# Expert tiles that gather their own token rows, begun four blocks earlier at five per block

## The chip, the cores and the metric

The kernel runs on one core of a Trainium2 chip. Its time is the device time of one execution in microseconds (us); the time before is the median of three runs. The core's engines are TensorE (PE, matrix products and transposes), VectorE (DVE), ScalarE (ACT), GpSimd (POOL) and the queue engine SyncE (SP). Each takes its own instructions in order and waits on semaphores that the others raise. TensorE's clock is granted at one of two levels, 1.2 and 2.4 GHz; the profile shows the granted share, 1.0 being 2.4 GHz.

## What is computed

```
xn = layernorm(x)                               # x: (2, 4096, 256) f32
out = x + mamba(xn) + moe(xn)

mamba: r = xn * rsqrt(mean(xn^2) + eps) * norm_w
       x_s, z = split(r @ in_proj.T)            # 512 channels each
       u = silu(causal_conv4(x_s) + conv_b)
       dt, B, C = split(u @ x_proj.T)           # 16 states
       delta = softplus(dt @ dt_proj.T + dt_b)
       h_t = exp(delta_t * A) * h_(t-1) + delta_t * u_t * B_t      # for each t, channel, state
       y = (C_t . h_t + u * D) * silu(z);  out_proj(y) + xn

moe:   logits = xn @ gate.T                     # 8 experts, hidden 512
       the two best experts of each token, each with a masked softmax weight
       moe = sum over the two of weight * w2 @ (silu(w1 @ xn) * (w3 @ xn))
```

All is f32. There are 8192 tokens, 64 tiles of 128.

## The kernel before

**Blocks.** The sequence is cut into blocks of 256 tokens, `(j, b)` with j = 0 to 15 and b the batch, 32 in all, numbered `number(j, b)` = 2j + b. A block has 32 steps v: a step handles one state s and one half of the channels. Blocks 0 to 7 and 28 to 31 are written out, those between are one hardware loop (`run`) whose round is two blocks. At each step ACT makes `exp(delta * A)` for the next step (`make_da`, two buffers), POOL makes `du * B` three steps ahead (`make_dbu`, a ring of eight), DVE scans (`scan`, two instructions of 256), PE transposes the states two steps behind (`transpose_h`) and DVE adds them, weighted with C, four steps behind (`add_state`).

**Work beside the steps.** The projections of the next block and the output of the block before stand at fixed steps of the `SLOTS` table, on each engine between the instructions of the recurrence: z at 0 and 1, y at 4 and 5, the output product at 8, `xs` at 10 and 12, two convolution pairs at 13 and 15, x_proj at 18, dt at 20 and 21, softplus from 22 to 28. POOL's part of the softplus (`w_minus_1` and `correction` at step 26, `make_delta` and `make_du` at 28) must end before the first `make_dbu` of the next block (at 29). `residual` on ACT (step 9) scales a second copy of the raw x block; SP loads it by `reload_x`, at step 8. `result` on DVE (step 11) adds that to the output product.

**Experts, routing.** In block 0, `normalise_all` on DVE makes the layer norm of all 64 token tiles in SBUF (`xall`): eight pairs before the first scan (NPRE), the other 24 one pair a step; `dispatch_T` (PE, ACT) transposes each tile and `dispatch_logits` makes its logits. At block 1, step 3 (ROUTE), `route` and `place` on DVE choose two experts per token and give each of the 16384 (token, choice) pairs a slot in an order sorted by expert, padded so that each tile of 128 slots has one expert. `eid` holds the expert of each slot tile. 135 tiles can be in use.

**Experts, dispatch.** From block 1, step 8 POOL sends one token tile each step by an indirect DMA (`dispatch`, L432) into `xbuf` in DRAM, 128 in all; with each row go the token's number and its weight. `xbuf` was filled with empty rows before (`clear`, 68 stores), as was the expert output `moe_dram` (33 stores).

**Expert tiles.** `tiles_at` places 12 tiles in two blocks (PER), from block 6 on (J0 = 3) to block 28. A tile that starts at step t has its transpose at t (XT), its copy and H1 at t + 2, H3 at t + 3, tanh at t + 4, DVE's two products (`tile_a2`, `tile_ha`) and Y at t + 5, the weighted copy (YO) at t + 7, and at t + 9 an adding indirect DMA on POOL to `moe_dram` (L445). Before it, `load_tile` on SP has brought its rows and their `meta` from `xbuf`; `load_weights` brings the expert's weights for the tile four further on. The weights lie where `xall` was. `add_result` on POOL at last adds `moe_dram` to `out`, one block each third step from block 28, step 26.

**Parameters.** ACT's queue loads all small weights; the two bias rows `dt_b` and `conv_b` are loaded element by element into a row of `dtT`. DVE's first product on a weight (L1064) waits for all nine of these loads.

## Time and profile before

| | us |
|---|---|
| median of 3 runs (lowest, highest) | 2923.68 (2920.98, 2927.97) |
| the profiled execution | 2921.28 |
| its span, first to last instruction | 2919.5 |
| PE busy, weight loads busy | 2437.7, 2049.5 |
| DVE busy | 2467.5 |
| ACT busy | 1504.8 |
| POOL busy | 2001.6 |

The predictions' sums are made against the profiled execution. A busy time is the union of an engine's instructions; on PE they are pipelined and overlap. In the rows below, a group row gives the line, engine and operation, out<-in with shapes and count, then busy time and mean ns of one, then the idle time just before them and what ended it. A timeline row gives start, duration, engine, line and operation, and in brackets the idle time before it and what ended that. The lines are those of the kernel printed above.

### The profile page before, as it was taken

The page shows a single profiled execution, that of the slowest core. Times are in us where ns is not written, and L with a number is a line of the kernel's source. Part 1 is how long each engine was busy: PE and PEld are TensorE (multiplying, and loading weights), DVE is VectorE, ACT ScalarE, POOL GpSimd, SP SyncE. Part 2 cuts the span into 40 slices and gives each one's busy share as a digit, 9 for nine tenths or more (in the row PEclk, how much of TensorE's full clock was granted, in tenths as well). Part 3 has the DMA queues.
Part 4 walks back from the last instruction along what each step waited for, and adds up shares of the span by engine and source line. Part 5 has one row for each costly group of instructions (what it writes and reads, how often), then busy time and mean ns, then how long its engine had stood idle before and what let it go on. Part 6 is the DMA issues. An engine that isn't in the chain of part 4 may idle for free.

```text
span 2919.5 us, 50661 instructions
## 1 busy us (share of the span) xinstructions
PE 2437.7 (83%) x14442; PEld 2049.5 (70%) x14442; DVE 2467.5 (85%) x3901; ACT 1504.8 (52%) x3675; POOL 2001.6 (69%) x1467
## 2 busy tenths in 40 slices
PE   2876655579999899999999989899898999997775
PEld 2864544458788778787778877788787777775554
DVE  6979777798899888898888898888898887998997
ACT  1444444455555555455555555555465554565553
POOL 3346999985777766677766777666676666777873
PEclk8757766779999999999999999999999999997776
DMA  7442432244565555464555565555564554542431
GB/s 219 120 106 80 155 104 75 75 143 129 161 180 148 158 168 156 143 189 142 163 162 148 160 174 158 155 167 147 159 174 137 168 163 147 175 119 53 78 75 36
DMA packets 316127, 406.46 MB, mean 139 GB/s; under 512 B 44296, under 2 KB 207496, under 8 KB 315800
## 3 DMA queue, kind: packets, MB, share of 16 engines
q1 hardware_dynamic: 284448, 359.49, 40.3%
q0 software_dynamic: 28144, 43.01, 8.1%
q8 instruction: 133, 2.18, 0.3%
q14 instruction: 194, 1.59, 0.2%
q10 hardware_dynamic: 3208, 0.19, 0.1%
HBM read 332.59 MB, written 78.39 MB: 141 GB/s over the span
## 4 chain that ended last, share of the span: by engine, by line
PE 48%; POOL 16%; DVE 15%; issue 11%; DMA 4%; ACT 4%; SPq 2%; ACTq 0%; DVEq 0%; POOLq 0%
PE HT L1246 9%; POOL h L468 7%; DVE h L1015 6%; PE G L1288 5%; PE G L1295 5%; PE FA L1205 4%; PE FB L1205 4%; PE G L1302 4%; DVE yT L1030 3%; DMA xraw<-in_x_dram 3%; PE FA L1172 3%; POOL xbuf L432 3%; PE FA L1311 2%; PE FB L1172 2%; POOL tmpA L476 2%
## 5 line engine op out<-in xcount | busy, mean ns | idle before, releaser
L468 POOL TENSOR_TENSOR h<-du,bbc 128x512 f32<-128x512 f32 x1024 | 1356.8, 1412 | 786.9 <-PE HT L1246 750.2
L1015 DVE TENSOR_TENSOR_SCAN h<-DA,carry,h 128x256 f32<-128x256 f32 x2048 | 1416.5, 733 | 196.1 <-ACT DA L716 83.5
L716 ACT ACTIVATE DA<-delta,alog 128x256 f32<-128x256 f32 x2048 | 891.4, 469 | 589.2 <-DVE h L1015 516.1
L1246 PE MATMUL HT<-ident,h 128*128 128x128 f32 x4096 | 687.8, 302 | 356.0 <-DVE yT L1030 329.1
L1246 PEld LDWEIGHTS HT<-ident,h 128*128 128x128 f32 x4096 | 514.9, 154 | 502.0 <-issue 359.1
L1030 DVE SCALAR_TENSOR_TENSOR yT<-HT,cT,yT 128x512 f32<-128x512 f32 x960 | 698.2, 727 | 187.8 <-PE HT L1246 187.3
L1288 PE MATMUL G<-xtT,W 128*128 128x128 f32 x2160 | 287.8, 290 | 0.0
L1288 PEld LDWEIGHTS G<-xtT,W 128*128 128x128 f32 x2160 | 274.5, 206 | 2.9
L1295 PE MATMUL G<-xtT,W 128*128 128x128 f32 x2160 | 263.8, 275 | 0.0
L1302 PE MATMUL G<-W,fill 128*128 128x256 f32 x1080 | 257.7, 381 | 3.3 <-DVE fill L991 3.3
L1295 PEld LDWEIGHTS G<-xtT,W 128*128 128x128 f32 x2160 | 252.8, 192 | 0.0
L445 POOL DMA_INDIRECT moe_dram<-W,meta x135 | 213.8, 1584 | 21.2 <-issue 18.6
L1302 PEld LDWEIGHTS G<-W,fill 128*128 128x128 f32 x1080 | 194.6, 190 | 28.0 <-DVE fill L991 4.9
L1172 PE MATMUL FB<-xrT,inT 128*128 128x256 f32 x512 | 154.1, 455 | 11.3 <-DVE inT L1064 11.3
L476 POOL TENSOR_SCALAR tmpA<-tmpB 128x1024 f32<-128x1024 f32 x32 | 129.7, 4054 | 42.0 <-ACT tmpB L690 42.0
L432 POOL DMA_INDIRECT xbuf<-W x128 | 129.7, 1013 | 21.3 <-issue 19.9
L1172 PEld LDWEIGHTS FB<-xrT,inT 128*128 128x128 f32 x512 | 115.5, 233 | 30.7 <-DVE inT L1064 11.7
L1311 PE MATMUL FA<-outT,zs 128*128 128x256 f32 x512 | 130.1, 412 | 0.8 <-DVE zs L1046 0.8
L1205 PE MATMUL FB<-xs,cwd 128*128 128x256 f32 x512 | 127.7, 391 | 0.0
L1205 PE MATMUL FA<-xs,cwd 128*128 128x256 f32 x512 | 127.7, 391 | 0.0
L1172 PE MATMUL FA<-xrT,inT 128*128 128x256 f32 x512 | 123.3, 384 | 0.0
L1311 PEld LDWEIGHTS FA<-outT,zs 128*128 128x128 f32 x512 | 104.7, 210 | 17.2 <-DVE zs L1046 1.0
(169 smaller groups left out, 2694.7 us busy)
## 6 DMA issues: line engine op xcount, KB each, us to landing
W<-in_w_T_dram SPq DMA_DIRECT2D x405, 512.0 KB, 4.9
bbc<-b_dram SPq DMA_DIRECT2D x256, 256.0 KB, 5.2
xbuf<-fill SPq DMA_DIRECT2D x68, 258.0 KB, 8.5
W<-xbuf SPq DMA_DIRECT2D x135, 128.0 KB
xraw<-in_x_dram SPq DMA_DIRECT2D x64, 256.0 KB, 6.3
W<-in_x_dram SPq DMA_DIRECT2D x32, 256.0 KB, 7.1
out_dram<-tmpA SPq DMA_DIRECT2D x32, 256.0 KB
moe_dram<-fill SPq DMA_DIRECT2D x32, 256.0 KB
```

The lines of the kernel that those rows point to most:

```text
L432: pool.indirect_dma_start(xbuf[:, :], bass.IndirectOffsetOnAxis(ap=slot[:, i:i + 1], axis=0), xall[:, i % TILES, :], None).then_inc(s_disp ...
L468: pool.tensor_tensor(h[:, v % RING], du[:, b, 2 * q:2 * q + 2, :], bbc[:, s // 2 % BRING, s % 2, :].unsqueeze(1).to_broadcast([P, 2, T]), ...
L716: i = act.activation(DA[:, v % 2, k, :], delta[:, b, c, :], ACT.Exp, scale=nega[:, c, s:s + 1])
L1015: i = dve.tensor_tensor_scan(h[:, v % RING, k, :], DA[:, v % 2, k, :], h[:, v % RING, k, :], carry[:, b, s, c:c + 1], ALU.mult, ALU.add)
L1030: i = dve.scalar_tensor_tensor(out=yT[:, b, k, :], in0=HT[:, k, :], scalar=cT[:, b, k, s:s + 1], in1=yT[:, b, k, :], op0=ALU.mult, op1=ALU ...
L1172: i = pe.matmul(dst[:, c, :], inT[:, k, at:at + P], xrT[:, b, k, :], start=(k == 0), stop=(k == KD - 1))
L1205: i = pe.matmul(dst, cwd[:, c, k, :], xs[:, c, k:k + T], start=False, stop=(k == TAPS - 1))
L1246: i = pe.transpose(HT[:, k, c * P:(c + 1) * P], h[:, (2 * s + c // 2) % RING, c % 2, k * P:(k + 1) * P], ident[:, :])
L1288: i = pe.matmul(G[:, 0, f * P:(f + 1) * P], w1[:, k % WSLOTS, c, f * P:(f + 1) * P], xtT[:, c, :], start=(f == 0 and c == 0), stop=(c == K ...
L1295: i = pe.matmul(G[:, 1, f * P:(f + 1) * P], w3[:, k % WSLOTS, c, f * P:(f + 1) * P], xtT[:, c, :], start=(f == 0 and c == 0), stop=(c == K ...
L1302: i = pe.matmul(G[:, 0, 0:DM], ha[:, f * P:(f + 1) * P], w2[:, k % WSLOTS, f, :], start=(f == 0), stop=(f == IC - 1))
L1311: i = pe.matmul(FA[:, t, :], zs[:, c, t * P:(t + 1) * P], outT[:, c, :], start=(c == 0), stop=(c == CH - 1))
```

## The change

The tokens' rows are no longer sent to `xbuf`. The normalised rows, each with the token's two weights, are stored in order to `xn_dram` (eight stores of 1 MB), and each tile gathers its 128 rows from there. For that the kernel inverts the slot table: slot = 128 * hi + lo; for each of the 128 (tile, choice) columns q DVE makes a one-hot row of lo (128 wide) and a one-hot row of hi (136 wide) times the token number, and PE accumulates their product over all q in PSUM, so that entry (lo, hi) holds the token number plus one, plus 8192 for a second choice, and 0 for an empty slot. Seven small DVE operations make indices and first/second masks of it. POOL copies each tile's index column (`choose`), gathers (`gather`, an indirect DMA with a read index) and later scatters by the same column. ACT makes each tile's weights from two 1-wide products.

The tiles begin in block 2 (J0 = 1), five a block (PER = 10 in two blocks), with five weight buffers instead of four; the last five tiles stand in block 28. All stages shift: index 0, gather 1, transpose 5, H1 7, H3 8, tanh 9, products and Y 10, YO 12, scatter 14. The hardware loop now runs 12 rounds (j = 2 to 13) instead of 10. `reload_x` moves from step 8 to step 6. `normalise_all` moves from DVE to ACT, with two pairs ahead of the first step. The two bias rows are loaded by SP after `in_proj`, and DVE's first product waits for `norm_w` only. `add_result` starts at block 29, step 18, each second step.

```diff
@@ constants
-    ZSTEP = 2
+    ONEHOTS = 8
-    J0 = 3
-    PER = 12
-    WSLOTS = 4
+    J0 = 1
+    PER = 10
+    WSLOTS = 5
-    META = 4
+    META = 5
-    NPRE = 8
-    LOW_TILES = TILES + TILES // 2
+    NPRE = 2
...
-        ADD_FROM = 26
+        ADD_FROM = 50
...
-            return at // 3 if at >= 0 and at % 3 == 0 and at // 3 < 2 * JB - 1 else None
+            return at // 2 if at >= 0 and at % 2 == 0 and at // 2 < 2 * JB - 1 else None
...
-        XT, XT_COPY, H1, H3, TANH, A2, MULT, Y, YO, SCATTER = 0, 2, 2, 3, 4, 5, 5, 5, 7, 9
-        W1_LOAD, W3_LOAD, W2_LOAD = 6, 7, 9
+        INDEX, GATHER = 0, 1
+        XT, XT_COPY, H1, H3, TANH, A2, MULT, Y, YO, SCATTER = 5, 7, 7, 8, 9, 10, 10, 10, 12, 14
+        W1_LOAD, W3_LOAD, W2_LOAD = 11, 12, 14
@@ SP
+            sp.wait_ge(s_id, 10)
+            sp.dma_start(cb_row.rearrange("o (c p) -> o c p", p=P),
+                         conv_b.rearrange("p c -> c p").unsqueeze(0), allow_slow_non_contiguous=True).then_inc(s_bias, 16)
+            sp.dma_start(dtT[ROWS:KDT, :].rearrange("o (c p) -> o c p", p=P),
+                         dt_b.rearrange("p c -> c p").unsqueeze(0), allow_slow_non_contiguous=True).then_inc(s_bias, 16)
             load_all(1)
...
+            def store_normalised():
+
+                sp.wait_ge(s_gate, 2)
+                for g in range(TILES // 8):
+                    sp.dma_start(xn_rows[g], xall[:, 8 * g:8 * g + 8, :]).then_inc(s_xnd, 16)
...
-                    if v == SLOTS["transpose"] and prv:
+                    if unit(j, b, v) < TILES // ZROWS:
+                        clear(unit(j, b, v))
+                    if due("normalise", v - 1) and prv:
                         reload_x(*prv)
...
+                    if unit(j, b, v) == U + ROUTE + 1:
+                        store_normalised()
+                        sp.wait_ge(s_xnd, 16 * (TILES // 8))
+                        sp.wait_ge(s_slot, 1)
+                        for g in range(WSLOTS):
+                            first_weights(g)
@@ POOL
-            def dispatch(i):
...
+            def choose(g, r):
+
+                if isinstance(g, int) and g == 0:
+                    pool.wait_ge(s_idx, 1)
+                pool.tensor_copy(token[:, r:r + 1], at_col(index, g)).then_inc(s_ix, 1)
+
+            def gather_ready(g):
+                pool.wait_ge(s_ix, g + 1)
+                if not isinstance(g, int) or g > 1:
+                    pool.wait_ge(s_xtr, g - 1)
+                    pool.wait_ge(s_gt, 2 * (g - 1))
+
+            def gather(g, k):
...
+                pool.indirect_dma_start(xt[:, k % 2, :], None, xn_dram[:, :],
+                                        bass.IndirectOffsetOnAxis(ap=token[:, k % META:k % META + 1], axis=0)).then_inc(s_xt[k % 2], 16)
...
                     if at := tiles_at(j, b, v, SCATTER):
                         scatter_ready(at[0])
+                    if at := tiles_at(j, b, v, GATHER):
+                        gather_ready(at[0])
...
-                    i = unit(j, b, v) - U - DISPATCH
-                    if 0 <= i < 2 * TILES:
-                        dispatch(i)
+                    if at := tiles_at(j, b, v, GATHER):
+                        gather(at[0], at[1])
+                    if at := tiles_at(j, b, v, INDEX):
+                        choose(at[0], at[1] % META)
@@ ACT
+            def normalise_all(i):
+
+                for q in range(NT * i, NT * i + NT):
+                    act.activation(xall[:, q, 0:DM], xall[:, q, 0:DM], ACT.Identity, bias=at_col(nm, q),
+                                   scale=at_col(rstd, q)).then_inc(s_nrm, 1)
...
+                    act.activation(weight[:, r, 0:1], xt[:, k % 2, DM + 1:ROW], ACT.Identity,
+                                   scale=at_col(second_of, g)).then_inc(s_gt, 1)
+                    act.wait_ge(s_gt, 2 * g + 1)
+                    act.activation(weight[:, r, 1:2], xt[:, k % 2, DM:DM + 1], ACT.Identity, bias=weight[:, r, 0:1],
+                                   scale=at_col(first_of, g)).then_inc(s_gt, 1)
@@ DVE
+            def invert():
+
+                for q in range(2 * TILES):
+                    wait(dve, s_inv, q - ONEHOTS + 1)
+                    dve.tensor_scalar(onehot[:, q % ONEHOTS, 0:P], its[:, 0:P], lo[:, q:q + 1], None,
+                                      ALU.is_equal).then_inc(s_oh, 1)
+                    dve.tensor_scalar(onehot[:, q % ONEHOTS, P:P + SLOTTED], its, hi[:, q:q + 1], tokv[:, q:q + 1],
+                                      ALU.is_equal, ALU.mult).then_inc(s_oh, 1)
+                dve.wait_ge(s_inv, 2 * TILES)
...
-            dve.wait_ge(s_par, NPAR)
+            dve.wait_ge(s_nw, 16)
...
                     if second(j, b) and v == ROUTE:
                         route()
                         place()
+                        invert()
@@ PE
+            def invert():
+
+                for q in range(2 * TILES):
+                    pe.wait_ge(s_oh, 2 * q + 2)
+                    pe.matmul(INV, onehot[:, q % ONEHOTS, 0:P], onehot[:, q % ONEHOTS, P:P + SLOTTED],
+                              start=(q == 0), stop=(q == 2 * TILES - 1)).then_inc(s_inv, 1)
```

## Rows read from the trace of the kernel before

**Rows 1.** The page: busy time by engine; TensorE's granted clock in 40 slices, tenths.

```profile
PE 2437.7 (83%) x14442; PEld 2049.5 (70%) x14442; DVE 2467.5 (85%) x3901; ACT 1504.8 (52%) x3675; POOL 2001.6 (69%) x1467
...
PEclk8757766779999999999999999999999999997776
```

**Rows 2.** Timeline of DVE: `result` (L1054) of blocks 0, 1, 4 and 27.

```profile
252.15 0.68 DVE L1054 TENSOR_TENSOR tmpA<-FA,xraw 128x512 f32<-128x512 f32 x1
...
337.94 0.68 DVE L1054 TENSOR_TENSOR tmpA<-FA,xraw 128x512 f32<-128x512 f32 x1
...
610.67 0.68 DVE L1054 TENSOR_TENSOR tmpA<-FA,xraw 128x512 f32<-128x512 f32 x1
...
2622.12 0.68 DVE L1054 TENSOR_TENSOR tmpA<-FA,xraw 128x512 f32<-128x512 f32 x1
```

**Rows 3.** Groups of instructions: the scans, the state sums, a tile's second product.

```profile
L1015 DVE TENSOR_TENSOR_SCAN h<-DA,carry,h 128x256 f32<-128x256 f32 x2048 | 1416.5, 733 | 196.1 <-ACT DA L716 83.5
...
L1030 DVE SCALAR_TENSOR_TENSOR yT<-HT,cT,yT 128x512 f32<-128x512 f32 x960 | 698.2, 727 | 187.8 <-PE HT L1246 187.3
...
L991 DVE TENSOR_TENSOR fill<-fill,G 128x512 f32<-128x512 f32 x135 | 92.8, 688 | 18.2 <-PE G L1295 5.6
```

**Rows 4.** Stretches: block 0, routing, six tiles, none: us, busy (count), clock, DMA, GB/s.

```profile
90.00:100.00 10.00, 10.00 (x51) 10.00 (x50) 10.00 (x17) 5.26 (x13) 2.54 (x2) 0.50 0.46 123
...
196.00:233.00 37.00, 3.83 (x21) 3.25 (x21) 33.67 (x107) 4.76 (x10) 4.38 (x4) 0.57 0.00 0
...
839.00:926.00 87.00, 81.35 (x516) 70.14 (x515) 76.12 (x118) 48.58 (x119) 60.67 (x44) 0.96 0.58 164
...
2758.00:2833.00 75.00, 56.18 (x261) 42.13 (x261) 67.80 (x105) 40.35 (x101) 58.42 (x48) 0.77 0.39 72
```

**Rows 5.** Timelines of SP, ACT, DVE around step 10 of block 14.

```profile
1380.07 0.37 SPq L306 DMA_DIRECT2D xraw<-in_x_dram  x1
...
1387.45 1.09 ACT L598 ACTIVATE xraw<-xraw,nm,onep 128x256 f32<-128x256 f32 x2 [5.06 <-DMA xraw<-in_x_dram]
...
1389.34 1.39 DVE L1015 TENSOR_TENSOR_SCAN h<-DA,carry,h 128x256 f32<-128x256 f32 x2 [2.11 <-ACT DA L716]
```

**Rows 6.** Timelines of PE in block 13 and DVE in block 14, steps 13 to 18.

```profile
1307.92 1.95 PE L1295 MATMUL G<-xtT,W 128*128 128x128 f32 x16
...
1310.42 2.00 PE L1205 MATMUL FB<-xs,cwd 128*128 128x256 f32 x8
...
1405.94 0.75 DVE L1030 SCALAR_TENSOR_TENSOR yT<-HT,cT,yT 128x512 f32<-128x512 f32 x1 [3.51 <-PE HT L1246]
...
1413.64 0.75 DVE L1030 SCALAR_TENSOR_TENSOR yT<-HT,cT,yT 128x512 f32<-128x512 f32 x1 [3.11 <-PE HT L1246]
```

**Rows 7.** POOL: ends of its chain in block 16; groups of its indirect DMAs.

```profile
1606.79 4.23 POOL L476 TENSOR_SCALAR tmpA<-tmpB 128x1024 f32<-128x1024 f32 x1
...
1621.09 2.50 POOL L468 TENSOR_TENSOR h<-du,bbc 128x512 f32<-128x512 f32 x2 [0.43 <-ACT carry L723]
...
L445 POOL DMA_INDIRECT moe_dram<-W,meta x135 | 213.8, 1584 | 21.2 <-issue 18.6
...
L432 POOL DMA_INDIRECT xbuf<-W x128 | 129.7, 1013 | 21.3 <-issue 19.9 <-POOL tmpA L481 0.6 <-POOL W L430 0.3
```

**Rows 8.** Start and block 0: DVE and SP timelines; last, who waited for whom.

```profile
27.75 1.42 DVE L1064 TENSOR_SCALAR inT<-inT,nw 128x1024 f32<-128x1024 f32 x2 [15.77 <-DMA dtT<-in_conv_b_dram]
...
31.28 0.39 DVE L1071 TENSOR_SCALAR xpT<-xpT 128x64 f32<-128x64 f32 x3
...
71.72 7.08 DVE L875 TENSOR_SCALAR W<-W 128x256 f32<-128x256 f32 x16
...
80.02 0.70 DVE L875 TENSOR_SCALAR W<-W 128x256 f32<-128x256 f32 x2
...
8.58 22.08 SPq L348 DMA_DIRECT2D W<-in_x_dram  x24
...
ACT W L567 <- PE G L1154: 53.1, 25, 5.3
```

More of the change, by code:

```diff
@@ L184, in build @@
         gate = scratch[1][:, 0:2 * TILES]
-        slot = scratch[6][:, 512:512 + 2 * TILES].bitcast(mybir.dt.uint32)
+        onehot = W[:, part + 4 * 1024:part + 4 * 1024 + ONEHOTS * (P + SLOTTED)].rearrange("p (r c) -> p r c", r=ONEHOTS)
+        hi, lo, tokv = [scratch[1][:, at:at + 2 * TILES] for at in (128, 256, 384)]
+        hi_i = scratch[1][:, 512:512 + 2 * TILES].bitcast(mybir.dt.int32)
+        slot_i = scratch[1][:, 640:640 + 2 * TILES].bitcast(mybir.dt.int32)
+        its = scratch[2][:, 0:SLOTTED]
+        idxf, index, second_of, first_of = [scratch[0][:, at * SLOTTED:(at + 1) * SLOTTED] for at in range(4)]
+        index = index.bitcast(mybir.dt.uint32)
+        INV = G[:, 1, 0:SLOTTED]
         LG = G[:, 1, :].rearrange("p (t e) -> p t e", e=E)
@@ L583, in normalise @@
                 act.wait_ge(s_x, 16 * (n + 1))
-                if isinstance(n, int) and n == EARLY:
-                    act.wait_ge(s_stats, LATE_MOMENTS + NEWTON + FINISH)
                 wait(act, s_delta, n)
@@ L738, in front @@
                 ln_dt(j, b)
-            for dst, src in ((nw, norm_w), (dpar, D_par)):
-                act.dma_start(dst[:, :], src).then_inc(s_par, 16)
+            act.dma_start(nw[:, :], norm_w).then_inc(s_nw, 16)
             act.dma_start(cw[:, :, :], conv_w.rearrange("(c p) o k -> p c (o k)", p=P)).then_inc(s_par, 16)
@@ L761, in _ @@
             make_da((0, 0), 0)
+            act.wait_ge(s_stats, LATE_MOMENTS + NEWTON + FINISH)
+            for i in range(NPRE):
+                normalise_all(i)
             def step(j, b):
@@ L870, in tables @@
                 chain(dve.tensor_scalar(onep[:, to], yy[:, 0, to], 1.0, None, ALU.add))
-            def normalise_all(i):
-                for q in range(NT * i, NT * i + NT):
-                    dve.tensor_scalar(xall[:, q, 0:DM], xall[:, q, 0:DM], at_col(mean, q), at_col(rstd, q),
-                                      ALU.subtract, ALU.mult).then_inc(s_nrm, 1)
             done = 0
@@ L931, in route @@
                 link(dve.reciprocal(gate[:, :], twice))
-                link(dve.tensor_copy(xall[:, :, DM + 1], gate[:, 0:TILES]))
+                for w in range(2):
+                    dve.wait_ge(s_route, done)
+                    dve.tensor_copy(xall[:, :, DM + w], gate[:, w * TILES:(w + 1) * TILES]).then_inc(s_gate, 1)
             def place():
@@ L964, in place @@
                 link(dve.tensor_reduce(where, rank.rearrange("p (e q) -> p q e", e=E), AX.X, ALU.add))
-                dve.tensor_copy(slot[:, :], where).then_inc(s_slot, 1)
-                its = scratch[2][:, 0:SLOTTED]
+                link(dve.tensor_copy(slot_i, where))
+                link(dve.tensor_single_scalar(hi_i, slot_i, 7, ALU.logical_shift_right))
+                link(dve.tensor_copy(hi, hi_i))
+                link(dve.scalar_tensor_tensor(out=lo, in0=hi, scalar=-float(P), in1=where, op0=ALU.mult, op1=ALU.add))
                 dve.wait_ge(s_iota, 2)
                 cmp = W[:, part + 5 * 1024:part + 5 * 1024 + SLOTTED * E].rearrange("p (i e) -> p i e", e=E)
+                link(dve.tensor_copy(tokv, tokens[:, :]))
                 link(dve.tensor_copy(its, eid[:, :]))
@@ L1091, in _ @@
             tables(EARLY * NT, TILES)
-            for i in range(NPRE):
-                normalise_all(i)
             def step(j, b):
```

137 lines of the change are left out of this document (58 added, 79 removed).

## The prediction

> **What bounds the kernel now.** I read the page first, then the length of a block, then single steps. The page [rows 1] has VectorE (DVE) busy 85% and TensorE (PE) 83% of the span, neither full. DVE's `result`, once per block, cuts the run [rows 2]: four blocks with dispatch take (610.67 - 252.15) / 4 = 89.6 us, the 23 up to 2622.12 take 2011.5, 87.5 each (six expert tiles; 88.1 without the first, which began late), and the last four steps of this clock take 288. A block without tiles is 75 us [rows 4]. A tile thus costs 13.1 / 6 = 2.2 us.
>
> Step by step (a block has 32 steps, one per scan pair) most steps last exactly what DVE needs: two scans and one `add_state`, 1.94 us from start to start [rows 3]. So DVE's order is the path, and a block is 32 x 1.94 = 62, nine other DVE operations of 0.6 = 5.4, six tiles x 1.4 for their two products [rows 3] = 8.4, together 75.9, and some 12 us of named stalls:
> - At step 10 the scan waits 2.11 us for ACT, which sat 5.06 us at `residual` until `xraw` had landed; SP had issued it 7.4 us before [rows 5]. About 1.6 a block on average (odd blocks lose 1.2).
> - At steps 16 and 18 `add_state` waits 3.51 and 3.11 for PE's transposes, which stand behind a convolution pair (2.55 per channel, 5.1) and a tile's H3 (1.8) [rows 6].
> - At the end POOL's chain of six operations sets the next scan: 1606.79 to 1622.4 = 15.6 [rows 7].
> Every second block adds about 3 more where the hardware loop closes.
>
> **The change, part by part.** The sum goes against the profiled execution: 2921.28 us, span 2919.5; the median of the runs shown is 2923.68, 2.4 above it.
>
> *Start.* The two bias rows go from ACT's queue to SP's, and DVE waits for `norm_w` alone. Before, DVE idled 15.8 us for them [rows 8]. That isn't all won: SP must now issue some 7 us of tiny rows ahead of 30 loads of x, whose 24 last took it 22.08 us [rows 8], so the statistics end not before about 46 instead of 54.7. At most 8.7; it could also cost 7, if the bias rows land late for the first convolution. I take 5. Sixteen normalisations leave DVE before the first scan (7.08 [rows 8]); four take their place on ACT at 0.5 each (two in 1.00, 1387.45 to 1388.45 [rows 5]), and the logits chain starts earlier by about 3.5. In block 0, 60 normalisations (30 us) come to ACT; they lie beside 53.1 us in which ACT waited for PE's transposes [rows 8]. PE is 100% busy there at a granted clock of 0.50, its 1.2 GHz level [rows 4], so PE, not DVE, sets that block, and nothing is won by freeing DVE. Some steps had no such wait: I charge 1.5 (0 to 8). Together -7 (-16 to +8). The lighter clearing (34 stores for 101) lies in SP's slack: 0.
>
> *Block 1.* Routing keeps its 37 us of DVE alone [rows 4] plus five small operations (1.2). The inversion is new: 128 pairs of DVE comparisons, 128 and 136 wide, with one and two per-partition scalars, and one f32 product each on PE; nothing else of the recurrence runs beside it, since DVE takes its orders in turn. One-scalar price: 1.42 / 2 = 0.71 for 1024 wide; three of 64 take 0.39, or 0.13 each [rows 8], so 0.6 ns an element, and 128 wide is 0.71 - 0.54 = 0.18. Two-scalar price: 0.70 / 2 = 0.35 for 256 wide, less 120 elements = 0.28. Sum 0.46 x 128 = 59. PE at its low clock makes 51 passes in 10.00 us [rows 4]; two passes a product, a little wider, are 0.42, 54 us, hidden just under DVE. Ends: 0.13 each gives 33; 0.44 each (16 in 7.08) gives 113; I take 59 as the nearest forms give it. With the 1.8 of the tail: +62, less 1.5 of dispatch before `result`: +60. SP meanwhile waits for 8.5 MB of stores and issues 7.9 MB of weights. At 200 GB/s that is some 82 us after the gates at 217, hence about 299, and the inversion ends near 295: hidden, barely.
>
> The Trainium skill (VectorE: DVE Perf Modes, The TRN2 errata) charges an SBUF operation 58 cycles plus half its f32 width, and nothing for scalars read per partition; by it the pair is 0.26 us and the inversion 33. The three narrow operations above start about 0.10 apart, where it says 0.094, so for immediates the trace agrees; the wider rows with such scalars lie above it, which is why the sum does not use it.
>
> *Block 1 to block 2.* 85.8 before [rows 2]. Dispatch (24 to 32 operations a block of 1.013 and their gaps [rows 7]) is gone, one tile's product comes: 75 + 2.5 = 77.5, so -8.3.
>
> *Blocks 2 to 28, five tiles each.* Four terms against the mean of 88.0:
> - `reload_x` moves two steps up, before the tile's weights: issue to residual grows from 7.4 to about 12 us, the wait goes. -1.6. Next late is PE's output product, which just fits.
> - PE: tiles now run H1/H3 at 7/8, 13/14, 19/20, 26/27, 0/1. A step's transposes may start 2.5 us late before `add_state` notices. At step 13 stand H1 and a convolution pair, 0.44 + 1.8 + 5.1 on a backlog of 1: stall at 16 +0.7. H3 no longer stands at 18: -1.6. At steps 0 and 1 H1, H3 and z together need 8 us against 3.9 + 2.5: just late, but the old stall there goes, -0.7 in all with small change. -1.6.
> - DVE: outside steps 26 to 31 four tiles' products before and after: 0. Inside, one pair (1.4) goes, but POOL sets that stretch.
> - POOL: gather and scatter both fall on step 26, behind the two long operations and ahead of the products that the next block needs. A gather's issue is unknown: 1.01 (plain) to 1.58 (adding) [rows 7]; I take 1.1. 1.1 + 1.58 + gaps = +2.9 on the chain; the scatter that stood ahead of it at 25 (1.57) goes, and the rest is slack of the chain: the stretch goes from 17.2 to 18.2, +1.0.
> Sum -2.2, less 0.5 since fewer bursts meet the loop's end: 85.3. Bounds: 83 (the chain hides the gather) to 88 (nothing but the reload gained, gather at 1.58 and late for PE). 26 such intervals to block 28's `result`: 26 x 85.3 = 2218 against 2622.12 - 337.94 = 2284.2: -66 (-126 to +4). The two extra loop rounds are in it. The choosing copies on POOL (0.3, five a block) and ACT's two 1-wide products per tile (0.6) lie beside waits; without cover 5 x 0.9 = 4.5 a block.
>
> *End.* One more tile's remains in blocks 28 and 29 and adds packed at every second step: 288 becomes 292.5, +4.5.
>
> Sum: -7 + 60 - 8.3 - 66 + 4.5 = -16.8: span 2902.7, execution 2904.5, and about 2906 beside the median. About 0.2% (6 us) is what a measurement can tell from no change.
>
> **Rivals.**
> - *Work is conserved (slower).* 135 tiles cost 2.2 wherever they stand, and POOL's gather on the end-of-block chain gives back what the reload wins, so blocks stay at 88: 26 x 88 = 2288, +4 instead of -66; total about 2976. For it: the tile's cost is mostly DVE's own 1.4, and POOL's chain is tight. It decides from 86 us a block (26 x 0.7 = 18). Against: the reload's wait is plain.
> - *Bursts were the cost.* With 5 tiles PE needs 5.5 less a block and its stalls at 16 and 18 shrink to those of a bare block: 82.7 a block, total about 2838. For: PE 81 busy of 87 [rows 4]. Against: 13/14 meets both convolutions.
> - *Dear inversion.* 0.44 an operation, as when POOL worked beside DVE [rows 8]: +54, total about 2960. Against: POOL is idle here.
> - *Cheap inversion.* 0.13 an operation, as for immediates: 33, PE at full clock: about 2880. It is what the errata rule of the Trainium skill would give.
> - *Late gather.* Issued 7 us into step 26 it must land by PE's step 30, 6 us on; scatters took 6.5 to land. Each us late past PE's slack is 27 us. Counted in the 88. The Trainium skill (DMA: Bandwidth & Descriptors, Anatomy of one DMA) fits 2.0 us plus bytes, 2.3 here; no gather is in this trace.
>
> **How the numbers follow.** Forecast 0.42 (2882 to 2930), conserved 0.22, bursts 0.16, dear 0.08, cheap 0.12. Range 2850 to 2968. Faster: 0.42 x 0.75 + 0.16 + 0.12 + a little of conserved = 0.61; same 0.10; slower 0.29.
>
> **What would show it.** The gap between the routing and the next scan: 61 (right), 35, or 115. `result` to `result` 85.3 mean in the middle. ACT's wait for `xraw` near 0 and no scan stall at 10; 4.3 at 16, 1.5 at 18. POOL from the first long operation to the next block's first product 18 to 19 us. PE waiting for the gathered tile: none. Blocks at 88 or more, or an inversion over 80, make the forecast wrong.

## The result: slower, where the prediction said slightly faster

The changed kernel takes 2981.05 us (median of 4, 2972.32 to 2983.86), the kernel before 2924.52 (median of 4, 2920.98 to 2927.97): a ratio of 1.0191, 95% interval 1.0168 to 1.0215. The prediction was 2906, in a range of 2850 to 2968. The profiled execution of the changed kernel has a span of 2982.0 us, 62.5 above the 2919.5 of before.

### The profile page after: what moved, and what is told of

Read it like the earlier page. It is cut to its first block, busy times and chain, and to the rows that moved or that the text cites. A ratio compares the mean times of both kernels' runs of the same rounds, so it can differ in the third digit from the quotient of the medians.

```text
span 2982.0 us, 52444 instructions
## 1 busy us (share of the span) xinstructions
PE 2512.3 (84%) x14698; PEld 2146.5 (72%) x14698; DVE 2498.1 (84%) x4105; ACT 1595.0 (53%) x4009; POOL 2031.3 (68%) x1607
## 4 chain that ended last, share of the span: by engine, by line
PE 58%; POOL 18%; DVE 14%; issue 7%; ACT 2%; DVEq 0%; SPq 0%; POOLq 0%; DMA 0%; ACTq 0%
PE HT L1284 10%; PE G L1333 8%; DVE h L1055 7%; PE G L1340 6%; POOL h L477 6%; PE G L1347 5%; PE FB L1243 4%; PE FA L1243 4%; PE FB L1210 4%; PE FA L1356 4%; POOL tmpA L485 4%; POOL delta L496 2%; DVE yT L1070 2%; POOL tmpA L490 2%; PE G L1315 2%
## 5 line engine op out<-in xcount | busy, mean ns | idle before, releaser
L477 POOL TENSOR_TENSOR h<-du,bbc 128x512 f32<-128x512 f32 x1024 | 1370.7, 1456 | 815.4 <-PE HT L1284 754.6
L1284 PE MATMUL HT<-ident,h 128*128 128x128 f32 x4096 | 673.3, 295 | 318.0 <-DVE yT L1070 308.1
L1284 PEld LDWEIGHTS HT<-ident,h 128*128 128x128 f32 x4096 | 511.1, 151 | 442.2 <-issue 248.6
L1333 PE MATMUL G<-xtT,W 128*128 128x128 f32 x2160 | 358.1, 335 | 59.5 <-ACT xtT L634 59.5
L1333 PEld LDWEIGHTS G<-xtT,W 128*128 128x128 f32 x2160 | 339.8, 247 | 67.6 <-ACT xtT L634 65.9
L1340 PE MATMUL G<-xtT,W 128*128 128x128 f32 x2160 | 274.1, 282 | 0.0
L1340 PEld LDWEIGHTS G<-xtT,W 128*128 128x128 f32 x2160 | 265.4, 200 | 0.0
L454 POOL DMA_INDIRECT moe_dram<-W,token x135 | 217.9, 1614 | 37.2 <-issue 37.2
L445 POOL DMA_INDIRECT W<-xn_dram,token x135 | 139.6, 1034 | 20.9 <-issue 6.9
L1210 PE MATMUL FB<-xrT,inT 128*128 128x256 f32 x512 | 150.5, 447 | 0.8 <-ACT xrT L618 0.8
L648 ACT ACTIVATE fill<-G 128x512 f32<-128x512 f32 x135 | 80.1, 593 | 130.7 <-PE G L1333 130.7
L485 POOL TENSOR_SCALAR tmpA<-tmpB 128x1024 f32<-128x1024 f32 x32 | 116.6, 3643 | 31.2 <-ACT tmpB L711 31.2
L1210 PEld LDWEIGHTS FB<-xrT,inT 128*128 128x128 f32 x512 | 117.4, 238 | 20.2 <-issue 1.1
L1210 PE MATMUL FA<-xrT,inT 128*128 128x256 f32 x512 | 122.5, 382 | 0.0
L1356 PE MATMUL FA<-outT,zs 128*128 128x256 f32 x512 | 120.6, 390 | 0.8 <-DVE zs L1086 0.8
```

Of the source, the lines that this page charges most:

```text
L477: pool.tensor_tensor(h[:, v % RING], du[:, b, 2 * q:2 * q + 2, :], bbc[:, s // 2 % BRING, s % 2, :].unsqueeze(1).to_broadcast([P, 2, T]), ...
L485: pool.tensor_scalar(tmpA[:, :, :], tmpB[:, :, :], 1.0, -1.0, ALU.add, ALU.add).then_inc(s_wm, 1)
L1210: i = pe.matmul(dst[:, c, :], inT[:, k, at:at + P], xrT[:, b, k, :], start=(k == 0), stop=(k == KD - 1))
L1284: i = pe.transpose(HT[:, k, c * P:(c + 1) * P], h[:, (2 * s + c // 2) % RING, c % 2, k * P:(k + 1) * P], ident[:, :])
L1333: i = pe.matmul(G[:, 0, f * P:(f + 1) * P], w1[:, k % WSLOTS, c, f * P:(f + 1) * P], xtT[:, c, :], start=(f == 0 and c == 0), stop=(c == K ...
L1340: i = pe.matmul(G[:, 1, f * P:(f + 1) * P], w3[:, k % WSLOTS, c, f * P:(f + 1) * P], xtT[:, c, :], start=(f == 0 and c == 0), stop=(c == K ...
```

## The profile after

The page of the changed kernel, busy times and TensorE's granted clock, beside [rows 1]:

```profile
PE 2512.3 (84%) x14698; PEld 2146.5 (72%) x14698; DVE 2498.1 (84%) x4105; ACT 1595.0 (53%) x4009; POOL 2031.3 (68%) x1607
...
PEclk7759899999999999999999999999999999999876
```

VectorE does 31 us more, TensorE is busy 75 us more for 256 more matmuls. The same `result` operation as in [rows 2] (now L1094) of blocks 0, 1, 4 and 27, from VectorE's timeline, cuts the run as before:

```profile
298.84 0.68 DVE L1094 TENSOR_TENSOR tmpA<-FA,xraw 128x512 f32<-128x512 f32 x1
...
372.59 0.68 DVE L1094 TENSOR_TENSOR tmpA<-FA,xraw 128x512 f32<-128x512 f32 x1
...
637.24 0.68 DVE L1094 TENSOR_TENSOR tmpA<-FA,xraw 128x512 f32<-128x512 f32 x1
...
2678.35 0.68 DVE L1094 TENSOR_TENSOR tmpA<-FA,xraw 128x512 f32<-128x512 f32 x1
```

| part | before | after | change | forecast |
|---|---|---|---|---|
| start, blocks 0 and 1 up to the first `result` | 252.15 | 298.84 | +46.7 | -7 + 60 = +53 |
| first to second `result` | 85.8 | 73.75 | -12.0 | -8.3 |
| 26 intervals | 2284.2 | 2305.8 | +21.6 | -66 |
| from there to the end | 297.4 | 303.65 | +6.3 | +4.5 |
| sum | 2919.5 | 2982.0 | +62.5 | -16.8 |

Three of the four terms are right within 6.3 us, and together 8 below the forecast. (Of the first row's +46.7, the start and block 0 are -14.8 and block 1 up to `result` +61.5.) The 26 five-tile intervals are 88.7 us each instead of the 85.3 forecast: an error of +88, of +79 in all. The start of each scan places them within the block (means over blocks 7 to 27, us, worked out from the starts of all 1024 scan pairs; 23 of 32 steps of the changed kernel need 1.94 or 2.55, the rest hold waits and tile products):

| steps | before | after | change | forecast |
|---|---|---|---|---|
| 0 to 5 | 14.8 | 17.2 | +2.4 | -0.7 |
| 6 to 12 (second load of x) | 18.4 | 16.8 | -1.6 | -1.6 |
| 13 to 19 (convolutions) | 23.0 | 22.0 | -1.0 | -0.9 |
| 20 to 25 | 13.0 | 13.5 | +0.5 | 0 |
| 26 to 31 (POOL's chain, loop) | 18.8 | 19.2 | +0.4 | +0.5 |
| block | 88.0 | 88.7 | +0.7 | -2.7 |

So the reload, the convolutions and POOL's end came out as forecast, and the new block's beginning is 3.1 us dearer than forecast. What stands there, in POOL's timeline of the changed kernel at the end of block 14 and the beginning of 15:

```profile
1475.22 3.64 POOL L485 TENSOR_SCALAR tmpA<-tmpB 128x1024 f32<-128x1024 f32 x1
...
1481.46 1.06 POOL L445 DMA_INDIRECT W<-xn_dram,token  x1 [0.15 <-POOL tmpA L490]
1482.82 1.61 POOL L454 DMA_INDIRECT moe_dram<-W,token  x1 [0.30 <-issue]
...
1489.36 2.35 POOL L501 TENSOR_TENSOR du<-delta,u 128x1024 f32<-128x1024 f32 x1
1492.05 4.93 POOL L477 TENSOR_TENSOR h<-du,bbc 128x512 f32<-128x512 f32 x4 [0.34 <-POOL du L501]
```

VectorE at the same place: the first scan of the block waits for POOL, and the state sum (`add_state`) of step 3 waits for TensorE:

```profile
1493.42 1.39 DVE L1055 TENSOR_TENSOR_SCAN h<-DA,carry,h 128x256 f32<-128x256 f32 x2 [2.90 <-POOL h L477]
...
1503.00 0.75 DVE L1070 SCALAR_TENSOR_TENSOR yT<-HT,cT,yT 128x512 f32<-128x512 f32 x1 [2.36 <-PE HT L1284]
```

TensorE there (L1284 transposes the state, L1333 is H1, L1210 a half of `z`, L1340 H3):

```profile
1495.51 1.11 PE L1284 MATMUL HT<-ident,h 128*128 128x128 f32 x4 [4.21 <-DVE yT L1070]
1496.42 3.62 PE L1333 MATMUL G<-xtT,W 128*128 128x128 f32 x16
1499.83 2.69 PE L1210 MATMUL FB<-xrT,inT 128*128 128x256 f32 x8
1502.36 0.60 PE L1284 MATMUL HT<-ident,h 128*128 128x128 f32 x4
1502.79 1.95 PE L1340 MATMUL G<-xtT,W 128*128 128x128 f32 x16
1504.58 1.89 PE L1210 MATMUL FA<-xrT,inT 128*128 128x256 f32 x8
```

And the same stretch by windows (us, PE, PEld, DVE, ACT, POOL busy with counts, granted clock, DMA share, GB/s):

```profile
1491.00:1495.50 4.50, 0.29 (x3) 0.05 (x1) 2.08 (x4) 2.06 (x8) 4.16 (x4) 0.90 0.43 156
1495.50:1500.00 4.50, 4.49 (x21) 4.50 (x22) 4.50 (x8) 1.22 (x4) 3.91 (x5) 0.50 0.00 0
1500.00:1503.50 3.50, 3.50 (x20) 3.02 (x19) 1.14 (x2) 1.54 (x4) 3.25 (x3) 0.79 0.69 191
```

The block's end, where POOL sets the pace, leaves TensorE idle for 4.21 us; after that its granted clock is 0.50, the 1.2 GHz level, and H1, which five tiles a block put at step 0, takes 3.62 us instead of 1.95, the first half of `z` 2.69 instead of 1.89 and the transposes ahead of them 1.11 instead of 0.60. So the transposes of 1502.36 come 3.0 us later than at the full clock, and VectorE waits 2.36 for them. In the kernel before, H1 and H3 stand at steps 2 and 3. Over blocks 7 to 27 TensorE's idle time at steps 31, 0 and 1 is 2.0 us a block before and 5.5 after, and the mean granted clock at steps 0 to 3 is 0.93, 0.81, 0.82, 0.95 before and 0.82, 0.50, 0.50, 0.86 after.

The inversion, from the groups by line (its two one-hot operations and its products):

```profile
L1315 PE MATMUL G<-W 128*128 128x136 f32 x256 | 58.5, 339 | 10.9 <-DVE W L1003 10.9
L1003 DVE TENSOR_SCALAR W<-W 128x136 f32<-128x136 f32 x128 | 45.2, 353 | 0.0
...
L1001 DVE TENSOR_SCALAR W<-W 128x128 f32<-128x128 f32 x128 | 36.9, 289 | 0.0
```

They are pipelined: the first starts at 219.83 and the last operation of the tail ends at 280.9, 61.1 us in all; the pair comes every 0.455 us (forecast 0.46). The window of the inversion, TensorE at a clock of 0.96:

```profile
219.80:281.00 61.20, 58.46 (x256) 39.63 (x256) 60.40 (x265) 0.00 (x0) 0.00 (x0) 0.96 0.58 190
```

## The experiments

Each "before" of a run below is the kernel before on the same chip: 2919.36 for a1 to a4 and 2927.26 for b1, b2, c1 and d1 (one execution each), 2926.0 for e1, f1 and g1 and 2923.76 for h1 (7 each). Runs without an interval are one profiled execution each. Their totals carry a spread of some 10 us, nearly all of it before block 1: that block begins at 169.4 us in the changed kernel's profile and at 160.5 to 162.2 in a1 to a4, which are the same up to there. The blocks themselves repeat well: blocks 2 to 28 take 2390.0 in the changed kernel and 2389.1 and 2389.9 in a2 and d1, 2271.2 in b2 and 2271.4 in h1. So the readings below go by blocks. A tile's stage `s` falls on steps `s`, `s`+6, `s`+12, `s`+19, `s`+25 (modulo 32) with five tiles a block, and on `s`, `s`+5, `s`+10, `s`+16, `s`+21, `s`+26 with six. The table has the same ranges of steps as above.

| run | 0-5 | 6-12 | 13-19 | 20-25 | 26-31 | block | us |
|---|---|---|---|---|---|---|---|
| after | 17.2 | 16.8 | 22.0 | 13.5 | 19.2 | 88.7 | 2983.8 |
| a1 scatter at 18 | 17.0 | 16.8 | 22.0 | 13.5 | 17.8 | 87.0 | 2928.2 |
| b1 all stages later | 14.8 | 16.9 | 22.1 | 13.0 | 17.8 | 84.6 | 2868.5 |
| b2 same, gather at 1 | 14.4 | 16.8 | 22.1 | 13.0 | 18.0 | 84.2 | 2862.2 |
| a4 six tiles, block 6 on | 15.1 | 16.8 | 24.0 | 13.0 | 19.1 | 88.0 | 2898.4 |
| f1 same, gather at 15 | 15.5 | 16.8 | 24.0 | 13.0 | 18.8 | 88.1 | 2893.9 |
| c1 same, gather 8, scatter 29 | 16.3 | 17.0 | 23.8 | 13.1 | 19.1 | 89.3 | 2921.8 |
| e1 before, reload at 6 | 14.7 | 17.0 | 23.8 | 13.0 | 19.0 | 87.5 | 2905.9 |

**a1: the scatter off POOL's chain.**

```diff
-        XT, XT_COPY, H1, H3, TANH, A2, MULT, Y, YO, SCATTER = 5, 7, 7, 8, 9, 10, 10, 10, 12, 14
+        XT, XT_COPY, H1, H3, TANH, A2, MULT, Y, YO, SCATTER = 5, 7, 7, 8, 9, 10, 10, 10, 12, 18
```

> The changed kernel with one edit: each tile's scatter stands at stage 18 instead of 14, so that it falls on steps 18, 24, 30, 5 and 11 and no longer on step 26, between POOL's two long operations and the products that the next block needs. Theory (POOL's chain sets the end of a block): steps 26 to 31 shorten from 19.3 us by the scatter and its gap, 1.9, the block from 88.7 to 86.8, the whole by some 27 x 1.9 = 51 us, to about 2931. Rival (the work of a tile costs the same wherever it stands): the block stays within 0.3 us of 88.7 and the total within 8 us of 2982.

2928.2: near the theory's figure. Steps 26 to 31 are 1.5 us shorter, the scatter's issue less a little, and the block 1.75; blocks 2 to 28 are 49 us shorter. The whole is another 7 shorter than the changed kernel's profiled execution: 8.6 less ahead of block 1, where the edit does nothing, and 1.7 more in it. What stays is the beginning of the block. TensorE's timeline there still has an idle stretch and a slow H1 behind it:

```profile
1466.05 0.85 PE L1284 MATMUL HT<-ident,h 128*128 128x128 f32 x4 [2.74 <-DVE yT L1070]
1466.69 3.43 PE L1333 MATMUL G<-xtT,W 128*128 128x128 f32 x16
```

**a2: the reload back at its old step.**

```diff
-                    if due("normalise", v - 1) and prv:
+                    if v == SLOTS["transpose"] and prv:
```

> The changed kernel with the second load of x issued at step 8 again instead of step 6. Theory (the earlier load is worth what the scan of step 11 waited before): ACT waits 4 us for the load at step 9, the scan after step 10 starts 1.2 to 2.1 us late, and the total grows by 27 x 1.6 = 43 us, to about 3025. Rival (with the weights of the tiles loaded at other steps the load lands in time from step 8 too, or the wait hides behind PE): less than 10 us.

2977.43, no different: the theory fell. In the changed kernel SP issues the load 0.2 us after ScalarE has freed the buffer, at whichever step; it has no tile loads any more behind which it could stand. SP and ScalarE of this run:

```profile
1416.04 0.37 SPq L317 DMA_DIRECT2D xraw<-in_x_dram  x1
...
1422.78 1.08 ACT L611 ACTIVATE xraw<-xraw,nm,onep 128x256 f32<-128x256 f32 x2
```

Issue to use is 6.7 us and nobody waits; in [rows 5] the transfer had 7.4 us after its issue and was waited for 5.06 of them, since the issue itself came 7 us after the buffer was free. So the earlier step adds nothing to the change: the 1.6 us a block of steps 6 to 12 come already with the loads' move from SP to POOL's gather.

**e1: the reload edit alone, on the kernel before** (the reverse of the same lines).

> The kernel before the change, with one edit of the change alone: the second load of x is issued at step 6 of a block instead of step 8, ahead of the expert tile's loads on SP. Theory (the wait at step 10 came from SP, which stood at the tile's loads while the buffer had been free for 7 us; the changed kernel has no such loads on SP, so there the step doesn't matter): step 10 falls from 5.4 and 4.6 us to 3.3, 1.7 a block on average over 27 blocks, total about 45 below the kernel before, 2880 (2870 to 2895). Rival (the block is closed by POOL's chain and the loop, which take the gain back): less than 15 won, 2910 or more.

2905.91 against 2926.0, between the two figures; against the profiled execution of before, 2921.28, it is 15.4, of which blocks 2 to 28 hold 11.4. The step itself did what the theory says (3.33 us for 5.42 in even and 4.57 in odd blocks; SP issued the load at 1363.81, 0.2 us behind ScalarE, and the tile's load after it). But steps 13 to 19 rose from 23.0 to 23.8: while VectorE stood at step 10, TensorE had caught up ahead of the convolutions (in the kernel before it is idle for 0.44 us a block at steps 12 and 13, in e1 never). A block is 0.5 shorter, not 1.7, and 3 us of the difference are in block 0, where the edit does nothing.

**a3: 8 of 128 columns inverted.** Most tokens are missing from its lists; the tiles gather spare rows in their place.

```diff
-                for q in range(2 * TILES):
+                for q in range(8):
...
-                dve.wait_ge(s_inv, 2 * TILES)
+                dve.wait_ge(s_inv, 8)
...
```

> The changed kernel with 8 of the 128 columns of the slot table inverted; the other slots are left out and count as empty, so most tiles gather spare rows, at the same number of instructions and bytes. Theory (the inversion stands wholly on the path at 0.455 us a column): block 1 shortens by 120 x 0.455 = 55 us and nothing else changes, total about 2927. Rival (the stores of the normalised rows and the first weights are hidden only by the inversion, and come out when it goes): the gap closes by under 40 us, and the steps after it wait for SP's loads.

2938.13, 43 below the changed kernel's median. The gap between the scans of steps 3 and 4 of block 1, in which the routing and the inversion stand, falls from 103.7 to 49.6, 54.1 as the theory says. But block 1 as a whole falls by 34 to 36 (141.7 for 176.1 to 177.8), since the inversion hides something. VectorE and SP of this run, in block 1:

```profile
254.05 1.39 DVE L1055 TENSOR_TENSOR_SCAN h<-DA,carry,h 128x256 f32<-128x256 f32 x2 [19.99 <-ACT DA L737]
```

```profile
225.96 16.19 SPq L338 DMA_DIRECT2D W<-in_w_T_dram  x15
242.25 1.42 SPq L317 DMA_DIRECT2D xraw<-in_x_dram  x1
```

SP holds the stores of the normalised rows and fifteen loads of weights ahead of the reload; with the inversion gone, ScalarE and then VectorE wait 20 us for it. So some 20 us of the inversion lie beside what SP has to do there anyway, and a cheaper inversion alone wins less than it saves. The rival is half right: the loads came out, though the gap closed by more than its 40.

**a4: six tiles a block from block 6, as before the change; gather and inversion as changed.**

```diff
-    J0 = 1
-    PER = 10
-    WSLOTS = 5
+    J0 = 3
+    PER = 12
+    WSLOTS = 4
...
-    META = 5
+    META = 4
```

> The changed kernel with the old density: six tiles a block from block 6 on, four weight buffers, four index columns; gather, inversion and stages stay as changed. Blocks 2 to 5 then are bare, 75.2 us each instead of 87.3. Theory (what costs is what falls on the end of a block and on its cold start, not the number of tiles): in the blocks with six tiles one gather stands in POOL's chain and no scatter, H1 stands at step 1 beside z, and a block is 87 to 88; total 4 x 75.2 + 23 x 87.5 = 2313 against 2390 for blocks 2 to 28, so about 2905. Rival (a tile costs 2.2 to 2.7 us wherever it stands): 135 x 2.7 over 27 bare blocks, the same 2390, total within 12 us of 2982.

2898.44, as the theory says, and faster than the kernel before. Blocks 2 to 5 are free of dispatch and of tiles (73.5 each instead of 87.2), and the others are 87.7, exactly before's. The five-tile placing, as the changed kernel has it, costs 79 us in blocks 2 to 28 against the old density with the same parts (2390 for 2311).

**b1 and b2: everything behind the gather four steps later.** b1 has the gather at 5, b2 at 1 as in the changed kernel.

```diff
-        XT, XT_COPY, H1, H3, TANH, A2, MULT, Y, YO, SCATTER = 5, 7, 7, 8, 9, 10, 10, 10, 12, 14
-        W1_LOAD, W3_LOAD, W2_LOAD = 11, 12, 14
+        XT, XT_COPY, H1, H3, TANH, A2, MULT, Y, YO, SCATTER = 9, 11, 11, 12, 13, 14, 14, 14, 16, 18
+        W1_LOAD, W3_LOAD, W2_LOAD = 15, 16, 18
```

> Tile stages moved later by four steps, the gather to step 5 of a tile and the scatter to 18: at 5, 11, 17, 24, 30 and 18, 24, 30, 5, 11 of a block, H1 at 11, 17, 23, 30 and 4, so that neither transfer stands between POOL's two long operations at 26 and the next block's first product, and no expert matmul stands right behind the idle PE at step 0. Theory (the block's end is too long and leaves PE cold at the start of the next block; it is all that makes the five-tile blocks dear): against the run with the scatter alone moved (blocks 6 to 28 at 87.0) the gather's 1.06 goes and the late expert matmul of steps 0 to 3 (1.4 a block) too, block mean 84.5 (84 to 85.3), whole kernel about 2865 (2850 to 2885). Rival (a tile costs 2.2 to 2.4 us wherever it stands): blocks stay at 86.5 to 87.5, kernel 2915 to 2935.

> As the run with everything shifted, but with the gather left at step 1 of a tile, hence at step 26 of the block between POOL's long operations and the next products. Theory (gather's issue on the chain costs its own 1.06 us a block): 1.1 a block more than the shifted run, about 30 us in all. Rival (what matters is only the cold expert matmul behind the end, and POOL's millisecond is slack): within 5 us of the shifted run.

2868.46 and 2862.19. For b1 the theory's 2865 holds. Between a1 and b2 gather and scatter are at the same steps, so their difference, 2.7 us a block, is the place of the matmuls, copies, products and weight loads alone: 2.6 us in steps 0 to 5, 0.4 in 20 to 25, -0.2 in 26 to 31. In b2 TensorE's mean granted clock at steps 0 to 3 of blocks 7 to 27 is 0.95 to 1.0. For b2 the theory fell: blocks 2 to 28 are 8.8 us shorter with the gather on POOL's chain than without. That does not make the gather there free. Its steps 26 to 31 are 0.2 longer; but b1 has gather and scatter together at step 30, directly behind the chain, and steps 0 to 12 are 0.5 longer, and the token's copy stood ahead of its chain, whose first long operation took 4.20 us, for 3.64 in b2. No run has the gather in a place that costs nothing. The group of H1 in the changed kernel, in a1 and in b2 (busy, mean ns, idle before):

```profile
L1333 PE MATMUL G<-xtT,W 128*128 128x128 f32 x2160 | 358.1, 335 | 59.5 <-ACT xtT L634 59.5
```

```profile
L1333 PE MATMUL G<-xtT,W 128*128 128x128 f32 x2160 | 353.2, 333 | 58.5 <-ACT xtT L634 58.5
```

```profile
L1333 PE MATMUL G<-xtT,W 128*128 128x128 f32 x2160 | 303.7, 301 | 0.0
```

There are two slow H1 a block in the changed kernel: the one at step 0, and one at step 26, where TensorE also waits 2.2 us (59.5 / 27) for ScalarE's copy, which stands behind the block's long functions. TensorE's timeline at that step, in the changed kernel:

```profile
1479.13 3.79 PE L1333 MATMUL G<-xtT,W 128*128 128x128 f32 x16 [2.22 <-ACT xtT L634]
```

b2 still has one slow H1, at step 30 (3.21 us), but there VectorE waits for POOL anyway and it is free.

**c1 and f1: six tiles from block 6, with the transfers elsewhere.** c1 has PE's and VectorE's stages at the steps of the kernel before, f1 at those of a4.

```diff
+    META = 12
...
+        INDEX, GATHER = 3, 8
+        XT, XT_COPY, H1, H3, TANH, A2, MULT, Y, YO, SCATTER = 16, 18, 18, 19, 20, 21, 21, 21, 23, 29
+        W1_LOAD, W3_LOAD, W2_LOAD = 22, 23, 25
```

This is c1, added to a4's first three lines; f1 has 14, 15 in the first, 21, 23, 23, 24, 25, 26, 26, 26, 28, 30 in the second and 27, 28, 30 in the third.

> The changed kernel's gather and inversion, but tiles as before the change: six a block from block 6, PE's, DVE's and ACT's stages at the same steps as in the kernel before, the gather at 8, 13, 18, 24, 29 and 2 of a block, the scatter at 29, 2, 7, 13, 18 and 23, nothing of both at 26 to 28. Theory (POOL's end of the block is what the change lost, the rest of its blocks costs no more than before): blocks 6 to 28 at 86 (85 to 86.8), 1.7 below the run with the late placing alone (87.7), total about 2860 (2845 to 2880). Rival (the loop's end and PE set it): 87.5 as before, total 2893 to 2900.

> Six tiles a block from block 6 as in the run with the late placing alone, all stages of PE, VectorE and ScalarE at the same steps of a block as there, but with the gather at 15, 20, 25, 31, 4 and 9 of a block instead of 1, 6, 11, 17, 22 and 27: it is off POOL's chain at the block's end, and lies neither next to the scatter nor within three steps of the activation that it waits for. Theory (each transfer on the chain costs its issue time): blocks 6 to 28 at 86.6 instead of 87.7, total about 2873 (2862 to 2885). Rival (as when the gather alone was put back on the chain: no change, POOL's time turns up elsewhere): 2890 to 2902.

2921.77 and 2893.88: in both the theory fell. (In blocks 7 to 27 c1 takes 28 us more than a4.) In c1 gather and scatter both stand at step 29, directly behind the chain, where POOL has just made the first product of the next block. Its timeline at the end of block 14:

```profile
1423.35 1.27 POOL L477 TENSOR_TENSOR h<-du,bbc 128x512 f32<-128x512 f32 x1 [0.40 <-PE HT L1284]
1424.77 1.05 POOL L445 DMA_INDIRECT W<-xn_dram,token  x1 [0.15 <-issue]
1425.82 0.20 POOL L432 COPY token<-W 128x1 uint32 x1
1426.18 1.64 POOL L454 DMA_INDIRECT moe_dram<-W,token  x1 [0.17 <-issue]
1427.27 5.52 POOL L477 TENSOR_TENSOR h<-du,bbc 128x512 f32<-128x512 f32 x4
```

and VectorE, whose second scan of block 15 has to wait for the second product:

```profile
1429.24 1.39 DVE L1055 TENSOR_TENSOR_SCAN h<-DA,carry,h 128x256 f32<-128x256 f32 x2 [2.49 <-POOL h L477]
```

f1 avoids both, and is 4.5 us faster than a4, but not by the chain: its later stages leave block 6 with less work, 76.8 us for 84.9. Over blocks 7 to 27 it takes 1849.4 us for 1848.0: steps 26 to 31 become 0.3 shorter, steps 0 to 5 0.4 longer. So taking one gather of 1.06 off the chain wins nothing over the block, as in b1 and b2.

**d1: the bias rows back on ScalarE's queue, VectorE waiting for all constants.**

```diff
...
+            act.dma_start(dtT[ROWS:KDT, :].rearrange("o (c p) -> o c p", p=P),
+                         dt_b.rearrange("p c -> c p").unsqueeze(0), allow_slow_non_contiguous=True).then_inc(s_par, 16)
...
+            dve.wait_ge(s_par, NPAR)
...
```

> The changed kernel with the two bias rows back on ACT's queue and VectorE waiting for all constants before its product for inT, as before the change. Theory (the wait is what the start had won): VectorE stands still until about 27.5 instead of 11.5, statistics end about 54 instead of 42, first scan at 73 (71 to 75) instead of 60.3, total about 2993. Rival (as in the prediction: the x loads behind the bias rows bound the statistics, so the edit is worth 5): first scan at 65, total 2986.

2992.48, as the theory says, though its first scan is at 70.0, not 73. VectorE again stands in front of its product:

```profile
26.29 1.42 DVE L1104 TENSOR_SCALAR inT<-inT,nw 128x1024 f32<-128x1024 f32 x2 [14.72 <-DMA dtT<-in_conv_b_dram]
```

The wait is worth 9.6 us at the first scan (60.3 to 70.0); the other ten runs with the changed kernel's start have that scan at 57.7 to 61.3, so it is 9 to 12. From d1's 70.0 to the 78.7 of before 8.7 remain, of which the sixteen normalisations of [rows 8] took 7.1; no run takes these apart from the rest.

**g1: f1 with half of the inversion spread over blocks 1 to 5.** 64 columns stay in block 1; 4 go behind each step 15 and 17, 3 behind 25 and 30.

> As the run with six tiles from block 6 and the gather apart, but only the first 64 of the inversion's 128 columns in block 1; the other 64 in blocks 1 to 5, four each behind steps 15 and 17, three each behind 25 and 30, where VectorE waits in blocks without tiles. Theory (they fill idle time of VectorE: 1.2 to 2.1 us at 16, 18, 26 and 31): 64 x 0.46 = 29 go from the gap in block 1 and 4 to 10 come back, total 20 to 25 below that run, about 2850 if it comes to 2873. Rival (what VectorE waits for is PE or POOL, which the extra work delays in turn, or VectorE is slower beside POOL): less than 10 below it.

2902.21 (median of 4; ratio to before 0.9921, 0.9904 to 0.9937); its profiled execution, 2890.67, stands 3 us below f1's. The rival is right: block 1 became 26.4 us shorter and blocks 2 to 5 became 26.8 longer. Behind 15 and 17 the eight columns cost 0.7 instead of 3.7, as hoped. But behind step 30 three columns took 5.4 us. VectorE there, and POOL:

```profile
467.64 0.27 DVE L1015 TENSOR_SCALAR W<-W 128x128 f32<-128x128 f32 x1
467.83 1.37 DVE L1017 TENSOR_SCALAR W<-W 128x136 f32<-128x136 f32 x1
469.12 1.29 DVE L1015 TENSOR_SCALAR W<-W 128x128 f32<-128x128 f32 x1
470.34 1.30 DVE L1017 TENSOR_SCALAR W<-W 128x136 f32<-128x136 f32 x1
471.56 1.30 DVE L1015 TENSOR_SCALAR W<-W 128x128 f32<-128x128 f32 x1
472.78 0.34 DVE L1017 TENSOR_SCALAR W<-W 128x136 f32<-128x136 f32 x1
```

```profile
467.85 4.93 POOL L491 TENSOR_TENSOR h<-du,bbc 128x512 f32<-128x512 f32 x4
```

While POOL makes its four products, 1.23 us each, VectorE finishes exactly one of these narrow operations per product.

**h1: b2 with the eight columns that hide.** Steps 15 and 17 of block 1, four each.

> The best placing so far (five tiles a block, every stage of a tile behind the gather four steps later than in the changed kernel, the scatter at 18, the gather at 1), and eight of the inversion's 128 columns taken out of the gap in block 1 and put behind steps 15 and 17 of it, four each. Theory (the placing is worth 118 us to the changed kernel; columns behind 15 and 17 hide, since VectorE waits there for PE and POOL runs no long operation): gap 3.7 shorter, steps 15 to 18 of block 1 0.7 longer, total about 2859 (2853 to 2866), ratio to the kernel before 0.977. Rival (the one run at 2862 was a lucky one, as the run with six tiles and 2894 after 2898 says nothing of spread): 2870 to 2885. For the columns: where they run beside POOL's products they cost 1.3 us an operation, so steps 15 to 18 would be 4 longer or more.

2856.63 (median of 4), against 2923.76: ratio 0.977, interval 0.9745 to 0.9796, the fastest version. Steps 15 to 18 of block 1 are 12.60 for 11.95, so eight columns cost 0.65 there. It confirms the placing; the part of the columns (3 us) is too small to show in the total.

## Why the prediction was wrong

- **The start** (forecast -7) was right in kind and too cautious: the first scan came 18.4 us earlier, and block 0 was 3.6 longer, so -14.8. I took 5 for the bias rows, where d1 shows 9 to 12: SP issued them in 5.2 us, not 7, and the statistics ended at 41.9, not 46. Up to the first `result` start and block 1 together were 6.3 below the forecast.
- **The inversion** (59 + 1.8) measured 61.1. The one- and two-scalar prices, 0.18 and 0.28, were right (0.195 and 0.26 from start to start), and SP was hidden, as forecast, though not barely: it had issued the last of the tiles' weights at 249.3 and this landed at 259.2, where I had it busy to about 299, and a3 uncovers 20 us of it. TensorE's products, priced at the low clock, ran at 0.96. The cheap inversion is out. The rule behind it (the Trainium skill, VectorE: DVE Perf Modes, The TRN2 errata) gives 0.26 a pair, where this trace has 0.455.
- **Block 1 to block 2** (-8.3) was -12.0, and no run looked at why.
- **Blocks 2 to 28** (-66) are where the forecast fell, at +21.6. Of its four terms the reload's size was right, its reason wrong: the earlier step adds nothing here (a2), and alone it wins 0.5 of the 1.6 (e1); TensorE at the convolutions was right; POOL's end was right. The step that failed is this one: "At steps 0 and 1 H1, H3 and z together need 8 us against 3.9 + 2.5: just late, but the old stall there goes, -0.7". It priced them at the full clock. They stand behind an idle stretch that the forecast's own POOL term makes longer, and run at the 1.2 GHz level at first: 10.96 us from 1495.51 to the end of `z` at 1506.47, of which 2.98 are what the low clock adds to the rows above. Without these the rest is 8.0, as forecast, so the amount of work was right and the clock was missing, though in the trace of before it averages 0.81 already at steps 1 and 2. In steps 0 to 5 that gave +2.4 us a block instead of -0.7: step 3 is 2.6 longer beyond the products that moved there, and of the old stall at steps 0 and 1, put down as gone with 0.7, only 0.2 went. 26 x 3.1 = 81 of the 88 us. Moving the tile's matmuls away from there (a1 to b2) gives back 2.6 of it a block. That shows the place to be the cause; that the clock makes the stall there is read from the durations, since no run has the three groups together at the full clock.
- **POOL's term** had the right size (+0.4 against +0.5 with the loop's end), but took both issues as given: moving the scatter alone (a1) is worth 49 us, most of the 57 by which the change lost.
- **The rivals.** "Work is conserved" gave the nearest time, 2976 with blocks at 88, for a partly wrong reason: the same five tiles cost 84.2 in b2, so work isn't conserved, its place decides. The range ended at 2968, below this rival's 2976, to which it gave a chance of 0.22, and began at 2850, above the 2838 of "bursts". "Late gather" did not occur: no TensorE wait for a gathered tile shows in the groups of the changed kernel.

One reading of the prediction was off without weight: the 88.1 a block "without the first" comes out at 87.9, and the sum uses 88.0.

What stays open: why moving a gather off the chain wins nothing over the block (a4 to f1, b2 to b1), when moving the scatter wins 1.75 us a block, nearly all of its issue and gap (1.9). In b1 the other place costs something itself; for f1 no run tells where the 0.3 us go.

## What to carry to other kernels

Look at the granted clock behind each idle stretch of TensorE in the trace of before, and price what a new placing puts there at that clock: here the idle time at the block's turn grew from 2.0 to 5.5 us, and H1, put right behind it, took 3.62 us for 1.95. When a periodic placing changes its period, list every stage modulo the block and look for the two bad places, on the chain that closes the block and directly behind it; here four steps of shift and the scatter's move were worth 119 us (2390.0 to 2271.2 in blocks 2 to 28), twice the loss. An edit that takes a wait away must be followed to the next wait: in the kernel before, the reload's 1.7 us a block shrank to 0.5, since TensorE had used them to catch up.
